# Residual without its mean, output matrices centred on the chip, sums of squares on ScalarE: a two-layer model on one core

## The reference: what is computed

```python
x = x + layernorm(L0_attn(layernorm(x)))   # a linear recurrence with 16 states, and Dp * x
x = x + layernorm(L0_ffn(layernorm(x)))    # 8 experts, each takes the 512 tokens with its best scores
x = x + layernorm(L1_attn(layernorm(x)))   # rms norm, linear attention with a second-order expansion
x = x + layernorm(L1_ffn(layernorm(x)))    # 8 experts, each token takes its two best
```

## Time and profile before

| what | us |
| --- | --- |
| median of 3 runs (701.6 to 701.68) | 701.61 |
| the profiled execution | 703.21 |
| its span | 701.4 |
| VectorE, ScalarE, GpSimd busy | 421.7, 343.0, 310.7 |
| TensorE busy, mean granted clock | 514.5, 0.85 of full |
| results stage | 45.7 to 92.5 |
| search and lists | 92.5 to 132.4 |
| first experts (TensorE busy 76.7, GpSimd 79.6) | 132.4 to 242.7 |
| key pass | 242.7 to 334.2 |
| query pass | 334.2 to 437.7 |
| routing | 437.7 to 465.0 |
| second experts (TensorE busy 201.7, VectorE 99.9) | 465.0 to 672.3 |
| tail | 672.3 to 701.4 |

### The profile page before, as it was taken

One profiled execution on the slowest core, in us unless ns is written; L12 is line 12 of the kernel. 1 busy time (PEld: TensorE's weight loads), 2 busy tenths in 40 slices (PEclk: granted clock), 3 DMA queues, 4 the chain that ended last, 5 costly groups with the idle time before them and its releaser, 6 DMA issues.

```text
span 701.4 us, 13529 instructions
## 1 busy us (share of the span) xinstructions
PE 514.5 (73%) x3846; PEld 374.3 (53%) x3847; DVE 421.7 (60%) x1761; ACT 343.0 (49%) x724; POOL 310.7 (44%) x329
## 2 busy tenths in 40 slices
PE   1759521588758157878899994169999999999924
PEld 1447110356435023434334432159999999999911
DVE  4789768654312279897246878964455455545456
ACT  3815533344323034444357662246666666666525
POOL 3514300358878433342002112036676776667444
PEclk9976855599987569888899997569999999999966
DMA  7501263112333421100001010011111111111164
GB/s 187 138 0 48 79 274 147 28 41 44 42 47 39 100 100 32 32 0 1 1 1 31 16 31 21 24 22 48 46 49 45 49 49 45 49 43 52 35 230 141
DMA packets 47287, 42.22 MB, mean 60 GB/s; under 512 B 15345, under 2 KB 41322, under 8 KB 46730
## 3 DMA queue, kind: packets, MB, share of 16 engines
q1 hardware_dynamic: 31658, 25.35, 11.3%
q0 software_dynamic: 10368, 15.82, 10.1%
q10 hardware_dynamic: 5216, 0.52, 0.5%
HBM read 26.23 MB, written 15.30 MB: 59 GB/s over the span
## 4 chain that ended last, share of the span: by engine, by line
PE 48%; DVE 26%; issue 10%; POOL 6%; ACT 6%; DMA 3%; ACTq 1%; DVEq 0%; POOLq 0%; SPq 0%
PE bank L1916 18%; PE banks L1937 4%; PE bank L1937 4%; POOL sum_dram L683 3%; DVE st L1284 3%; PE bank L1774 3%; PE bank L1764 2%; PE bank L1729 2%; POOL arena L667 2%; DVE mv L1289 2%; DVE st L1014 2%; ACT arena L938 1%; POOL rstd L700 1%; PE bank L1830 1%; DVE hit L1147 1%
## 5 line engine op out<-in xcount | busy, mean ns | idle before, releaser
L1916 PE MATMUL bank<-arena 128*128 128x128 f32 x1136 | 140.9, 278 | 0.4 <-ACT arena L989 0.4
L1916 PEld LDWEIGHTS bank<-arena 128*128 128x128 f32 x1136 | 134.7, 195 | 0.7 <-ACT arena L989 0.7
L700 POOL TENSOR_TENSOR rstd<-ve,mhalf 128x4 f32<-128x4 f32 x40 | 48.8, 1219 | 167.6 <-DVE ve L1292 119.4
L1546 DVE TENSOR_TENSOR arena<-arena,bank 128x512 f32<-128x512 f32 x71 | 48.8, 688 | 82.4 <-PE bank L1916 82.4
L754 POOL DMA_INDIRECT y_dram<-arena,sidx x71 | 69.9, 985 | 44.9 <-DVE arena L1551 41.3
L975 ACT ACTIVATE arena<-wgu 128x1024 f32 x71 | 74.9, 1057 | 26.8 <-PE bank L1916 26.4
L746 POOL DMA_INDIRECT arena<-x3row_dram,gidx x71 | 68.8, 969 | 36.4 <-issue 21.0
L981 ACT ACTIVATE arena<-bank 128x512 f32<-128x512 f32 x71 | 42.4, 597 | 43.0 <-PE bank L1916 43.0
L667 POOL DMA_INDIRECT arena<-x1row_dram,idx x32 | 31.3, 979 | 43.8 <-DVE idx L1244 34.3
L683 POOL DMA_INDIRECT sum_dram<-arena,idx x28 | 44.2, 1577 | 10.9 <-issue 7.9
L1265 DVE TENSOR_TENSOR arena<-arena,bank 128x256 f32<-128x256 f32 x32 | 13.5, 422 | 57.3 <-ACT arena L870 57.3
(11 more groups left out here) (370 smaller groups left out, 1077.0 us busy)
## 6 DMA issues: line engine op xcount, KB each, us to landing
wgu<-in_wgu SPq DMA_DIRECT2D x1, 4096.0 KB, 12.4
wgu<-y_dram SPq DMA_DIRECT2D x8, 512.0 KB, 7.2
X<-in_x SPq DMA_DIRECT2D x8, 256.0 KB, 6.4
sum_dram<-zero POOLq DMA_DIRECT2D x8, 256.0 KB, 4.2
x1row_dram<-row SPq DMA_DIRECT2D x8, 256.0 KB, 2.4
w<-in_w SPq DMA_DIRECT2D x1, 2048.0 KB, 17.3
acc<-sum_dram SPq DMA_DIRECT2D x8, 256.0 KB, 2.9
w<-in_wd SPq DMA_DIRECT2D x1, 2048.0 KB, 9.9
```

The lines of the kernel that those rows point to most:

```text
L700: nc.gpsimd.tensor_tensor(out, ve[:, u], mhalf[:, 0:J], ALU.pow).then_inc(done, 1)
L1546: nc.vector.tensor_tensor(gl[:, m.pair], sgl[:, m.pair], bank[3 + m.pair][:], ALU.mult).then_inc(f_gated, 1)
L1916: last = nc.tensor.matmul(bank[first + m.pair][:, h * P:(h + 1) * P], wnow[:, m.pair, at_:at_ + P], xrT[:, m.ring], start=True, stop=True)
```

## The change

X keeps its rows without their mean. GpSimd subtracts the mean from X once, after the first normalisation; the means are kept in `mu` and added back by VectorE during the second expert stage. The matrices that end each sublayer are centred over their output features: wout and diagD by VectorE ahead of the scan, w2 by GpSimd during the search, wo by VectorE, wd by GpSimd, one expert ahead of each step of the query pass. So every sublayer's output has mean zero, all shifts (`nmr`, `shift1`, `shift2`) go, and ScalarE's normalisations are copies with a scale. A variance is then a mean of squares, and for one y in two of the results stage, for the sums of the first experts, for the last x3 and for all groups of the tail ScalarE makes it by four squarings with an accumulator; epsilon is added by VectorE or by GpSimd. The other statistics stay on VectorE. w2 is loaded first of the three expert matrices.

```diff
 # SyncE, behind the stored rows and scores
+            sp.dma_start(w2[:], inp["w2"]).then_inc(s_w2, 16)
+            sp.dma_start(w13[:], inp["w13"]).then_inc(s_w0, 16)
             sp.dma_start(wgu[:], inp["wgu"]).then_inc(s_w1, 16)
-            sp.dma_start(w13[:], inp["w13"]).then_inc(s_w0, 16)
-            sp.dma_start(w2[:], inp["w2"]).then_inc(s_w0, 16)
 # GpSimd, behind the first powers
+            nc.gpsimd.tensor_copy(mu_at, mvx[:, :, :, :, 0])
             for t in range(T // 4):
                 pool.dma_start(sum_dram...[t], zero[:]).then_inc(c_zst, 16)
             for c in range(CH):
-                for var, of, factor, done in ((a_yvar, vey, rstdy, a_yrstd), (a_x1var, ve, rstd, a_x1rstd)):
...
+                for b in range(NB):
+                    pool.wait_ge(a_xn, LEAD + c * 2 + b + 1)
+                    nc.gpsimd.tensor_tensor(Xv[:, c, b], Xv[:, c, b], mvx[:, c, b, :, 0:1].to_broadcast([P, J, D]),
+                                            ALU.subtract).then_inc(a_xc, 1)
+            for b in range(NB):
+                factor(a_yvar, vey, rstdy, 0, b, a_yrstd)
+            for c in range(CH):
+                for b in range(NB):
+                    at_least(pool, a_x1n, (c - 1) * 2 + b + 1)
+                    factor(a_x1var, ve, rstd, c, b, a_x1rstd)
+                    if c + 1 < CH:
+                        factor(a_yvar, vey, rstdy, c + 1, b, a_yrstd)
+            def centre(w, half, done):
+                n = D // 2
+                pc.mark(nc.gpsimd.tensor_tensor(half, w[:, :, 0:n], w[:, :, n:], ALU.add))
+                pc.wait()
+                while n > 1:
+                    n //= 2
+                    pc.mark(nc.gpsimd.tensor_tensor(half[:, :, 0:n], half[:, :, 0:n], half[:, :, n:2 * n], ALU.add))
+                    pc.wait()
+                pc.mark(nc.gpsimd.tensor_scalar(half[:, :, 0:1], half[:, :, 0:1], 1.0 / D, None, ALU.mult))
+                pc.wait()
+                nc.gpsimd.tensor_tensor(w, w, half[:, :, 0:1].to_broadcast([P, w.shape[1], D]), ALU.subtract).then_inc(done, 1)
+            pool.wait_ge(s_w2, LEAD + 16)
+            centre(w2[:].rearrange("p e h d -> p (e h) d"), part(0, E0 * D)..., s_wc)
...
+            def power_of_squares(out, u, wait, n, done):
+                pool.wait_ge(wait, LEAD + n)
+                pc.mark(nc.gpsimd.tensor_tensor(fv[:, u], fv[:, u], eps[:], ALU.add))
+                pc.wait()
+                nc.gpsimd.tensor_tensor(out, fv[:, u], mhalf[:, 0:J], ALU.pow).then_inc(done, 1)
 # GpSimd, query_pass
+                if n:
+                    pool.wait_ge(s_wc, LEAD + 1 + n.n)
+                    centre(wd[:, n.n], rank[:]..., s_wc)
                 if m:
                     power(rstd[:, m.b], m.b, q_yvar, m.n + 1, q_yrstd)
 # ScalarE, results stage
             for c in range(CH + 1):
+                if c < CH:
+                    act.wait_ge(a_y, LEAD + 2 * c + 2)
+                    at_least(act, a_yrstd, 2 * c)
+                    for j in range(J):
+                        last = squared(j, bank[YBANK[c % 2][1]][:, j * P:(j + 1) * P], vey[:, 1, j:j + 1])
+                    last.then_inc(a_ysq, 1)
                 if c:
...
-                            last = nc.scalar.activation(row[:, b, j], Xv[:, c - 1, b, j], ACT.Identity,
-                                                        bias=nmr1[:, b, j:j + 1], scale=rstd[:, b, j:j + 1])
+                            last = nc.scalar.activation(row[:, b, j], Xv[:, c - 1, b, j], ACT.Copy, scale=rstd[:, b, j:j + 1])
 # ScalarE, key_pass
                 evict(3)
+                if h:
+                    act.wait_ge(d_acc[h.b], LEAD + 16 * h.trip + 16)
+                    if not early(h, 2):
+                        act.wait_ge(d_frstd, LEAD + h.n - 1)
+                    squares_of(lambda j: acc[:, h.b, j], row, h.b, d_fvar)
                 if g:
-                    act.wait_ge(d_xnmr, LEAD + g.n + 1)
+                    act.wait_ge(d_xrstd, LEAD + g.n + 1)
 # VectorE, ahead of the scan
+            do(nc.vector.tensor_reduce(wout_sum[:], wout[:], AX.X, ALU.add))
+            for b in range(NB):
+                nc.vector.scalar_tensor_tensor(wout[:, b], wout_sum[:, b:b + 1].to_broadcast([P, P]), -1.0 / D, wout[:, b], ALU.mult,
+                                               ALU.add)
 # VectorE, results stage
+            def y_stats(c):
+                dve.wait_ge(a_y, LEAD + c * 2 + 1)
+                stats(lambda j: bank[YBANK[c % 2][0]][:, j * P:(j + 1) * P], 0, mvy[:, 0], vey[:, 0], a_yvar)
+                dve.wait_ge(a_ysq, LEAD + c + 1)
+                nc.vector.tensor_scalar(vey[:, 1], vey[:, 1], EPS, None, ALU.add).then_inc(a_yvar, 1)
+            y_stats(0)
             for c in range(CH):
                 for b in range(NB):
...
+                    dve.wait_ge(a_xc, LEAD + c * 2 + b + 1)
+                    dve.wait_ge(a_yrstd, LEAD + c * 2 + b + 1)
+                    for j in range(J):
+                        last = nc.vector.scalar_tensor_tensor(Xv[:, c, b, j], bank[YBANK[c % 2][b]][:, j * P:(j + 1) * P],
+                                                              rstdy[:, b, j:j + 1], Xv[:, c, b, j], ALU.mult, ALU.add)
+                    last.then_inc(a_yn, 1)
+                    if b == 1 and c + 1 < CH:
+                        y_stats(c + 1)
+                    dve.wait_ge(a_yn, LEAD + c * 2 + b + 1)
+                    stats(lambda j: Xv[:, c, b, j], b, mv[:, b], ve[:, b], a_x1var)
 # VectorE, key_pass
-                if h:
-                    dve.wait_ge(d_acc[h.b], LEAD + 16 * h.trip + 16)
-                    if not early(h, 2):
-                        dve.wait_ge(d_std, LEAD + h.n - 1)
-                    stats1(lambda j: acc[:, h.b, j], h.b, d_fvar)
-                if g:
-                    shift(g.b, d_xrstd, g.n + 1, d_xnmr)
 # VectorE, second experts
+                if m and early(m, GR):
+                    nc.vector.tensor_tensor(xl[:, m.n], xl[:, m.n], mu[:, m.n].unsqueeze(2).to_broadcast([P, J, D]), ALU.add)
 # VectorE, mix: the products nmr, shift1 and shift2 go; x3_shift goes; the last x3_stats goes to ScalarE
 # tail, VectorE
+                if m and m.n < BY_DVE:
+                    dve.wait_ge(g_y[m.n][0], LEAD + g_y[m.n][1] + 16)
+                    nc.vector.tensor_tensor(ysum[:, m.n, 0], ysum[:, m.n, 0], ysum[:, m.n, 1], ALU.add).then_inc(g_add, 1)
                 if l:
-                    dve.wait_ge(g_out, LEAD + l.n + 1)
+                    dve.wait_ge(g_rstd, LEAD + l.n + 1)
+                    for j in range(J):
+                        last = nc.vector.scalar_tensor_tensor(xl[:, l.place, j], ..., rstd[:, l.b, j:j + 1], xl[:, l.place, j], ALU.mult, ALU.add)
 # tail, ScalarE: squares_of(...) for each group; GpSimd: power_of_squares(...)
```

169 lines of the change are left out of this document (67 added, 102 removed).

## The result

The changed kernel takes 710.6 us (median of 4 executions, 707.9 to 713.3), the kernel before 701.6 in the same session: 1.0119 times, 95% interval 1.0086 to 1.0151. That is slower, by 9 us. Predicted were 713.8 us, within 702 to 724. The four times lie in two pairs, 707.9 and 708.4, and 712.8 and 713.3. The profiled execution is of the first pair (708.4, span 706.5), 2.2 us under its median, and the profiled execution of the kernel before took 703.2 (span 701.4), 1.6 over its median. So the stages of the two profiles add to +5.1 us and not to +9; how far the stages scatter is shown by the first experiment.

A forecast was written before the change was run, and what follows sets the result against it. Outside the expert stages no engine was taken as full: loops of hand-overs and queue order bound the kernel. Terms 1.0 + 1.5 + 1.0 + 6.0 + 3.0 + 2.0 - 2.3 = +12.2 us gave 713.8 us, range 702 to 724.

The forecast's parts named there:

- wout on VectorE: Opening: centring wout on VectorE just ahead of its chain, which waited for nothing, adds 1.0 us.
- X centred on GpSimd: Opening: GpSimd's eight subtractions of 1.28 us run to about 39 and hold VectorE's two-operand chain, +1.5 us (0 to 2.6).
- Results loop: Results stage: VectorE waits for ScalarE's squares behind score copies; turn 8.75 or 10.05 us against 8.3, +1.0 (-1.5 to +2.3).
- Search: Threshold search: VectorE's two-operand additions wait for GpSimd's long instructions centring w2, +6.0 us (0 to 11).
- Key pass: Key pass: ScalarE's squares stand between its last copy and the normalisation, +3.0 us (+1.5; with slower squares +6.5).
- Query pass: Query pass: centring wd[n] (4.6 us) delays the y power, turns of 11.5 us, +5.8; last steps give back 1.5.
- Second experts: Second expert stage: eight additions of the means, 0.7 us each, fall in VectorE's idle half, 0 us.
- Tail: Tail: TensorE is late next, then ScalarE's squares and a short chain end at 696.3 against 698.66, -2.3 us.
- The first (VectorE not held): Opening and search: GpSimd's wide instructions don't hold VectorE, so 1.5 and 6.0 us fall away: 706.3 us; chance 0.17.
- The second (GpSimd holds up nobody): GpSimd's centring: wd[n] takes 3.3 us, query part -4.5 us, no stalls: 699.8 us; chance 0.15.
- The third (slower GpSimd): GpSimd's centring: slower than assumed; at 7 us for wd[n] five turns grow by 2.4 each: 726 us; chance 0.13.
- The fourth (the loops don't stretch): Results and key loops: ScalarE's copies come earlier, so 1.0 and 3.0 us fall away: 709.8 us; chance 0.10.

The follow-up runs named there:

- the first experiment: The changed kernel run again without an edit: 711.9 to 713.8 us in five executions, ratio 1.0161 to the kernel before.
- the fifth experiment: Changed kernel, but VectorE makes the second y's statistics in the results stage, without ScalarE's four squares: 706.7 us, ratio 1.0083 to the kernel before.
- the seventh experiment: Changed kernel, but VectorE makes the statistics of the first experts' sums in the key pass, without ScalarE's squares: 709.2 us, ratio 1.0099.
- third: Changed kernel, but ScalarE instead of GpSimd centres w2 during the search: 707.0 us, ratio 1.009 to the kernel before.
- fourth: Changed kernel, but GpSimd centres w2 in pieces of two rows in the wide steps: 708.1 us, ratio 1.0094 to the kernel before.
- last experiment: Changed kernel, but the search's addition of the step to the candidates also writes an unread accumulator: 710.6 us, ratio 1.0104 to the kernel before.

## Why the prediction came out right, by its own steps

*wout on VectorE, +1.0.* 1.05. Right.

*X centred on GpSimd, +1.5 (0 to 2.6).* 0, the lower bound. The size of the instruction was off: 1.03 us, not 1.28; the second operand is repeated here, and with two full ones the same 512 elements took 1.25 (the first of the six additions at 103.05). So the eight ended 1.4 us ahead of the chain's first two-operand instruction. Whether VectorE would have been held there was not tried; in the search it was.

*Results loop, +1.0 (-1.5 to +2.3).* +1.75 in the profile, +1.0 to +3.3 over the others, a turn of 9.86 us, between the 8.75 and 10.05 that I gave for the two clocks and near the slower. The mechanism was the one named, and the fifth experiment shows it. The term that was short is the one from the end of the rows to the end of the score copies, 3.3 at full clock and 4.6 at half: it took 4.7, 4.8 and 5.1 us in the three turns (in the second at a granted clock of 0.64). I had taken the middle turn at full clock.

*Search, +6.0 (0 to 11).* +5.86, and without GpSimd's work 0. The mechanism is right, the agreement in size partly luck: I counted on the additions with two operands alone and on four of GpSimd's instructions (1.55 + 0.5 + 0.25 + 3.7). Held were one such addition (2.00) and twice the step with one tensor and one value per partition (0.80 and 3.08), which I had not expected to be held at all.

*Key pass, +3.0 (+1.5 to +6.5).* +0.18, and +0.2 to +2.5 over the other profiles, six of the eight with squares in place under the +1.5 that I gave as the lower end. This step failed in size. The step from ScalarE's last copy to the transposed copy was to grow from 22.3 us over seven turns to 24.7 or more; it took 22.3 again in the profile, and at most 23.2 in the others. Six turns took 3.37 us on average for my 3.65, most of it the squares with their hand-over, 1.07 for 1.30, since the first of them starts under the last copy; the seventh took 2.08 for 2.8. Beside the kernel before, the squares put 5.6 us more between copy and scaling over the seven turns, the scalings are 2.6 shorter, and ScalarE's waits for TensorE ahead of the transposed copy add to 6.9 us instead of 9.9. So the sum stood still. The squares do cost 2 to 3 us by the seventh experiment, but in the rest of the turns, from the transposed copy to the last copy, which I had left unchanged. It was 46.4 us before and 46.5 after, and is 42.6 to 45.7 where squares and shifts are both gone: unchanged, but by a gain and a loss that I did not have.

*Query pass, +5.8, then -1.5.* +5.91 and -0.39. The turn of 11.5 us is 11.52 measured (57.58 over five), one centring 4.3 for 4.6. The -1.5 was too much: the last two turns hardly got shorter by the missing shifts: 10.4 us each, 10.6 before. Routing -2.3: -2.50.

*Second experts, 0.* -1.1 in the profile, 0.0 to -1.3 over the others. Against one profile of before this may be scatter, as the -0.8 of the first experts.

*Tail, -2.3.* -3.8, over eleven profiles -2.3 to -4.9. TensorE was late next, as said. The chain behind it was right: 3.68 predicted, 3.76 measured. The rest is that TensorE itself starts earlier: its first sum begins 11.4 us behind the last scatter's issue instead of 12.5, which changes from profile to profile of the changed kernel as well (11.4 to 12.7) and follows the loads of the results.

The sum of +12.2 is +5.1 in the profile and +9 in the medians. The 7 us between forecast and profile: the key pass and what follows it 2.8 and 1.3, X 1.5, the tail 1.5, the two expert stages 1.9, less 0.75 in the loop and 1.1 in the last query turns, which were worse than forecast. That the medians come nearer, 9.0 against 12.2, is because the two profiled executions lie on opposite sides of their medians, 1.6 us over and 2.2 under, and no merit of the sum.

*The rivals.* The first (VectorE not held) is false: third, fourth and last experiment. The second (GpSimd holds up nobody) would have needed wd[n] in 3.6 us, and it took 4.3. That it isn't a question of the length alone but of the place I had not seen: behind the power of y the same 4.3 us cost 0.1 a turn. The third (slower GpSimd) is false by the same rows. The fourth (the loops don't stretch) holds in length for the key pass, though squares there cost 2 to 3 us against the same pass without them, and fails for the results stage.

## What to carry to other kernels

Work given to an engine with room is free only where its queue is idle and nothing behind it is due; look for the pause in the queue before the engine's average. Here one move past a single instruction was worth 5.5 us in five turns. Long GpSimd instructions beside short VectorE ones belong in pieces or on ScalarE. And before an instruction leaves a busy engine, ask who will wait for it where it goes: in the tail, where VectorE was full, the squares on ScalarE were worth 2 to 5 us, in the two loops, where it wasn't, they cost 2 to 4 us in the results stage and 2 to 3 in the key pass.
